# Selective-scan layer on one Trainium2 core: the stores of the scan's output are issued by ScalarE instead of SyncE

## What is computed

```python
def step(state, inp):
    d, b, c, uu = inp
    dA = jnp.exp(d[..., None] * A_neg[:, None, :, :])
    state = dA * state + (d * uu)[..., None] * b[:, :, None, :]
    y = jnp.einsum('kbcn,kbn->kbc', state, c)
    return (state, y)
```

## Time and profile before

| | us |
|---|---|
| median of 3 runs | 17231.57 |
| the profiled execution, its own time | 17236.15 |
| its span, first to last instruction | 17234.5 |

### The profile page before, as it was taken

How to read it: one execution, slowest core, us unless ns; L and a number is a source line. 1 busy time by engine, 2 the same in 40 slices (tenths; PEclk the granted TensorE clock), 3 DMA queues, 4 the chain that set the end, 5 groups by cost and what they waited for, 6 DMA issues and landing times. The chain is left out here.

```text
span 17234.5 us, 361490 instructions
## 1 busy us (share of the span) xinstructions
PE 12704.4 (74%) x127392; PEld 8742.7 (51%) x127392; DVE 11266.0 (65%) x10439; ACT 7765.1 (45%) x13769; POOL 6782.0 (39%) x3199
## 2 busy tenths in 40 slices
PE   7889999888999954454466666666666666667799
PEld 5666666666666632222244444444444444444477
DVE  5666666666666655555477777777777777775532
ACT  4444444444444434544455545554555545552200
POOL 1000000000000014423577777887778877772100
PEclk9999999999999977777677777777777777776799
DMA  5222222222222237766899999999999999998711
GB/s 124 65 57 58 59 59 53 66 56 66 59 59 59 53 106 186 179 153 159 209 233 233 234 230 233 235 235 234 236 232 235 237 228 232 233 230 222 197 39 40
DMA packets 2038805, 2633.89 MB, mean 153 GB/s; under 512 B 1083612, under 2 KB 1935324, under 8 KB 2013404
## 3 DMA queue, kind: packets, MB, share of 16 engines
q1 hardware_dynamic: 1991388, 2487.10, 59.5%
q0 software_dynamic: 12288, 86.71, 2.3%
q10 hardware_dynamic: 34944, 57.81, 1.2%
HBM read 2103.61 MB, written 556.32 MB: 154 GB/s over the span
## 5 line engine op out<-in xcount | busy, mean ns | idle before, releaser
L1731 DVE TENSOR_TENSOR_SCAN L2.h<-L2.ps,L2.db 128x912 f32<-128x912 f32 x2688 | 5515.0, 2056 | 1569.2 <-POOL L2.db L1587 1522.1
L1587 POOL TENSOR_TENSOR L2.db<-L2.du,L2.bt 128x896 f32<-128x896 f32 x2688 | 5580.1, 2096 | 1551.7 <-DMA L2.du<-du 1468.0
L1608 PE MATMUL L2.ps<-L2.dm,L2.wa 32*128 32x112 f32 x21504 | 2306.9, 346 | 2471.1 <-DVE L2.h L1731 2343.4
L1669 ACT ACTIVATE L2.ps<-L2.ps 128x896 f32<-128x896 f32 x2688 | 2424.5, 902 | 3503.4 <-PE L2.ps L1608 3501.6
L1608 PEld LDWEIGHTS L2.ps<-L2.dm,L2.wa 32*128 32x128 f32 x21504 | 1899.6, 246 | 3268.2 <-DVE L2.h L1731 2940.3
L1621 PE MATMUL L2.ps<-L2.h,L2.cd 128*8 128x96 f32 x50176 | 2575.6, 362 | 5.5 <-DVE L2.h L1731 5.5
L1621 PEld LDWEIGHTS L2.ps<-L2.h,L2.cd 128*8 128x8 f32 x50176 | 1439.4, 108 | 583.6 <-DVE L2.h L1731 5.6
L314 POOL TENSOR_TENSOR L1.x_res<-L1.x_res,L1.ob 96x3136 f32 (+1 forms) x16 | 95.4, 5977 | 2582.2 <-ACT L1.qv L457 2582.2
L314 POOL TENSOR_TENSOR L0.x_res<-L0.x_res,L0.ob 96x3136 f32 (+1 forms) x16 | 95.9, 6007 | 2367.8 <-ACT L0.qv L457 2367.8
L366 PE MATMUL L1.p_proj<-L1.xt,L1.w_hi 128*96 128x448 f32 x3024 | 826.4, 383 | 194.2 <-DVE L1.xt L560 167.5
L366 PE MATMUL L0.p_proj<-L0.xt,L0.w_hi 128*96 128x448 f32 x3024 | 826.3, 383 | 194.3 <-DVE L0.xt L560 167.6
(11 more groups left out here) (255 smaller groups left out, 19811.4 us busy)
## 6 DMA issues: line engine op xcount, KB each, us to landing
L2.du<-du SPq DMA_DIRECT2D x5376, 224.0 KB, 6.6
L2.dm<-d SPq DMA_DIRECT2D x896, 336.0 KB, 6.8
y<-L2.ysum SPq DMA_DIRECT2D x896, 84.0 KB
L0.left<-table SPq DMA_DIRECT2D x48, 1176.0 KB
L0.right<-table SPq DMA_DIRECT2D x48, 1176.0 KB
L1.left<-table SPq DMA_DIRECT2D x48, 1176.0 KB
L1.right<-table SPq DMA_DIRECT2D x48, 1176.0 KB
du<-L2p.work SPq DMA_DIRECT2D x64, 784.0 KB, 7.5
```

The lines of the kernel that those rows point to most:

```text
L1587: pool.tensor_tensor(db[:, n % RB, :, 2:ROW], du[:, n % RD, :].rearrange("p (c t) -> p c t", t=SPAN), row, ALU.mult)\
L1608: mm = pe.matmul(decays[n % RA][:, lo:lo + SPAN], wa[rows, u * QUAD + e, :], dm[rows, u * QUAD + e, :], start=True, stop=True)
L1669: act.activation(a, a, ACT.Exp).then_inc(a_ready, 1)
L1731: dve.tensor_tensor_scan(h[:, half, u * UNIT:(u + 1) * UNIT, :].rearrange("p c t -> p (c t)"), decays[n % RA], db[:, n % RB, :, :].rearran ...
```

## The change

The four stores of a half leave SP's program. ACT issues them on its own DMA queue at the end of its half-span, after the decay and the carry of unit 11 and ahead of `make_cd`. It first waits until its own seven copies have landed (`sum_out`). SP's wait on `sum_out` goes with the stores. Addresses, sizes and the semaphore `y_stored` stay as they are. The last store of the pass moves to the end of ACT's program.

```diff
@@ SP @@
-                    if u == 2 and earlier is not None:
-                        sp.wait_ge(sum_out, fills + (2 - FILLS))
-                        steady(sp)
-                        store_y(*earlier, half)
...
-            for half in range(2):
-                sp.wait_ge(sum_out, (DIRS * HALVES - 1 + half) * FILLS + 2)
-                store_y(DIRS - 1, NSPANS - 1, half)
@@ ACT @@
+            def store_y(k, s, half):
+                for q in range(4):
+                    at = s * SPAN + SPAN // 4 * q
+                    if k % 2:
+                        at = at * -1 + (TOK - SPAN // 4)
+                    rows = slice(at, at + SPAN // 4) if isinstance(s, int) else bass.ds(at, SPAN // 4)
+                    place = y_dram[k, :, rows, half * HALF:(half + 1) * HALF]
+                    act.dma_start(place, ysum[32 * q:32 * q + BATCH, half, :, :]).then_inc(y_stored[half], 16)
...
+                if not first:
+                    act.wait_ge(sum_out, before + (FILLS + 2))
+                    steady(act)
+                    if half:
+                        store_y(k, s, 0)
+                    elif begun:
+                        store_y(k - 1, NSPANS - 1, 1)
+                    else:
+                        store_y(k, act.snap(s - 1), 1)
                 if half == 0:
                     make_cd(k, s, before)
...
+            act.wait_ge(sum_out, DIRS * HALVES * FILLS + 2)
+            store_y(DIRS - 1, NSPANS - 1, 1)
```

More of the change, by code:

```diff
@@ L1499, in load_du, with half_span @@
                     sp.dma_start(du[:, slot, g * QUAD * SPAN:(g + 1) * QUAD * SPAN], src).then_inc(du_in[slot], 16)
[L1501 to L1510, removed]
+            def half_span(k, s, half, later, table):
                 units = count(sp, k, s, 2 * UNITS, half * UNITS)
-                fills = count(sp, k, s, 2 * FILLS, half * FILLS)
                 for u in range(UNITS):
@@ L1542, in span @@
             def span(k, s, last):
[L1543 to L1546, removed]
                 if last:
@@ L1550, in span @@
                     later = (k, s + 1) if isinstance(s, int) else (k, sp.snap(s + 1))
-                half_span(k, s, 0, earlier, (k, s), k if k and isinstance(s, int) and s == 0 else None)
-                half_span(k, s, 1, earlier, later, k + 1 if last and k + 1 < DIRS else None)
+                half_span(k, s, 0, (k, s), k if k and isinstance(s, int) and s == 0 else None)
+                half_span(k, s, 1, later, k + 1 if last and k + 1 < DIRS else None)
             sp.wait_ge(cleared, 1)
```

## The result

| | before | after |
|---|---|---|
| median of 13 runs | 17224.97 | 17148.3 |
| lowest to highest | 17209.45 to 17241.57 | 16911.1 to 17230.26 |
| the profiled execution, its own time | 17236.15 | 17109.6 |

The medians of the 13 runs have a ratio of 0.9955 and their means one of 0.9934 (0.990 to 0.997 with 95%); without the six runs that took over 1.5% more than the shortest, the ratio is 0.9895 (0.9862 to 0.9927), which favours a kernel whose runs scatter. The kernel is faster, by about 1% at most. The gain is 77 us in the medians and 126.6 us in the profiled executions, where 511 were forecast. A second thing is new: the runs of before lie within 0.2% of each other, those of after within 1.9%.

What follows compares the result with a forecast made beforehand. The du load was taken to bind, held by SP's queue blocked at stores. Loads 27.4 plus stores 1.8 gave 29.2 us a half-span, 2.3 less; 222 x 2.3 = 511 us off 17236 gave 16725, range 16300 to 17260.

Steps and rivals of the forecast that it cites:

- the bound and what held SP: Scan pass: du loads bind; SP's queue, blocked at stores, holds them back, 3.7 us behind a store.
- The third rival: Stores and loads: something both queues share is the block, so no change, 17236 us within 30; chance 0.12.
- ACT's side: ACT at a half's end: four issues, addresses and a wait take 2.3 us (1.4 to 3.4), costed at nothing.
- a sign: Trace of ACT's queue: its four store issues would take 2 to 3 us together.
- The cushion: ACT before unit 0's scan: 2.6 us of slack after a half 0; lateness at most 90 us over the pass.
- the store's own cost: DMA engines per half-span: the moved stores' bytes cost 0 to 2.4 us, taken as 1.8.
- The first rival: DMA engines: stores hidden at cost 0, half-span 27.4 us, program 16326 us; chance 0.15 for 16300 to 16590.
- the loads without the store: Half-span loads: 20.9 us for the mix at 245.5 GB/s plus 6.5 for eight du, together 27.4 us.
- the second rival: Smaller gain: stores cost 2.4 us or more, or ACT's hold eats part; chance 0.15 for 16860 to 17200 us.
- The fourth rival: The eight store engines: short writes between long reads lengthen loads; slower, 17570 us at 50 ns a packet; chance 0.11.
- the marks: Trace signs: du issues keep 2.85 us, slot waits rise, no share under 0.8, multiply's idle falls to about 960 us.

Runs made afterwards that it cites:

- even stores: Each y store takes 16 partitions, 8 of them unused rows: in the changed kernel (ACT's queue) 16419.08 us; in the kernel before (SP's queue) 17283.47 us.
- no stores: Changed kernel without any y store in the scan pass; ACT only counts the semaphore up and the next stage reads a stand-in: 16638.51 us, ratio 0.9666.
- half the bytes: Changed kernel with stores of 14 of the 28 tokens on 8 partitions, next stage reading a stand-in: 17346.7 us, ratio 1.0063.
- less in flight: Changed kernel, but SP waits for two more free slots, so at most four units of du are in flight instead of six: 17241.05 us, ratio 1.0011.
- waiting: Changed kernel, but SP waits once per half, ahead of its fifth unit, until ACT's stores have landed: 17483.54 us, ratio 1.0156.
- short reads: Kernel without stores, ACT issuing loads of the stores' size in 384-byte runs instead: 18097.28 us on 8 partitions, 17995.78 us on 16.
- tiny stores: Changed kernel with one token per store instead of 28, next stage reading a stand-in: 16604.54 us on 8 partitions, 16634.08 us on 16.

## Why the prediction was wrong in size

**Right: the bound and what held SP.** Before, the queue was blocked at the store. After, du's four issues keep their time beside the stores; SP's queue over a half-span, which answers the earlier trace rows:
```profile
14000.14 2.87 SPq L1499 DMA_DIRECT2D L2.du<-du  x4
...
14004.05 2.85 SPq L1499 DMA_DIRECT2D L2.du<-du  x4
...
14012.69 14.13 SPq L1499 DMA_DIRECT2D L2.du<-du  x10
...
14032.45 2.86 SPq L1499 DMA_DIRECT2D L2.du<-du  x4
```
The long entry in the middle contains waits for slots. The third rival, one block for both queues, is out, though 17148 us is only 88 us from its 17236. It had a page's rule beside it: by the Trainium skill (DMA: Bandwidth & Descriptors, section on issuing engines not being separate DMA queues) another issuing engine saves issue time alone. The gap between even stores on SP (17283) and on ACT (16419) disagrees, unless the time for which an issue stands blocked is counted as issue time: what the second queue saves is the blocking of the first, 5% of the time, though SP's unblocked issue time was never the bound.

**Right: ACT's side.** Its four issues were put at 2.3 us with bounds of 1.4 and 3.4. At the end of a half 0, in ACT's timeline, which answers the earlier trace rows:
```profile
10022.54 0.28 ACTq L1644 DMA_DIRECT2D y<-L2.ysum  x1
10022.94 0.20 ACT L1664 COPY L2.db<-L2.h 128x8 f32<-128x8 f32 x1
10023.00 2.85 ACTq L1644 DMA_DIRECT2D y<-L2.ysum  x3
10026.03 2.34 ACT L1651 ACTIVATE L2.cd<-L2.cc,L2.image 128x112 f32<-128x112 f32 x8 [2.90 <-issue]
10028.27 0.90 ACT L1657 ACTIVATE L2.ps<-L2.ps 128x896 f32<-128x896 f32 x1
```
From first start to last end it takes 3.1 us in the mean of all stores, within the bounds but over the 2 to 3 us named as a sign. The cushion held for the most part: the scan's idle time behind ACT rose from 29.2 us in sum (11.9 + 17.3) to 77.7 (40.4 + 37.3 above), 48 us in the whole pass where at most 90 were allowed.

**Within its bounds, but too high: the store's own cost.** It was bounded by 0 and 2.4 us and taken at 1.8. With even stores, twice the bytes, the half-span is 27.8 us; against the 27.4 worked out for the loads alone that leaves 0.4. The same 27.8 holds with the real stores while the engines are in step. No run gives the cost cleanly, since the kernel with no stores, 28.8 us, has its own late engine. The first rival's premise, hidden stores, comes nearest: it gave 16326, and 16419 was reached with even stores.

**Wrong: the loads without the store.** The step put du, dm, bt and cc at 245.5 GB/s, the rate of the earlier trace rows, and so at 20.9 us. After, the same mix runs at 214 in the mean of all half-spans: 5.13 MB / 214 is 24.0 us, 3.1 more. The packets that end from 10 to 22 us after a half-span's first scan carry, in GB/s (profiled runs, without the ends of each direction):

```
before 249, after 214, even stores 254, half the bytes 206, no stores 239, less in flight 246, waiting 247
```
With 24.0 for the mix, 6.5 for the other du and 0.4 for the stores that makes 30.9, and the half-span is 30.9 where 29.2 was forecast: the mix brings 3.1 us more and the stores 1.4 less. The difference of 1.7 us is 381 us over the pass, the amount by which the profiled execution falls short of the forecast (511 - 127 = 384). The row was read rightly, but it was a rate of engines that are in step, and what keeps them so, as far as the runs tell, is the very block that the change removes. I asked for each term what covers it, but not what keeps a rate as it is. What showed it in the trace of before was there: engines run dry at each store, and the store uses half of them.

**The rivals.** The time fell into the second rival's range, but not by its mechanism: neither the stores' price nor ACT's hold (48 us at most) ate the gain. The fourth rival had the place, the eight engines, and the mark that it was to be known by, a share near 1 with fewer GB/s. Its price was wrong: a turn between short writes and long reads would cost just as much on sixteen engines, where next to nothing is lost, and would fall in the stretch of the stores, which runs at 282 to 305 GB/s. Of the marks, no stretch looked at fell below a share of 1; the idle time ahead of the multiply came to 1347 where 960 was given (654 with even stores, 8588 to 14780 us).

**Shown, argued, open.** Shown: as many engines are late as a store has partitions (8, 12), also in loads that land after the stores; a half-span is 27.8 us in step and 30.5 to 32 out of step within one execution; emptying the queue, or making the stores even, restores step and rate. Argued only: that the eight late engines are the eight that store, since the trace doesn't name the engine of a landing; that the lag makes the loads slow and not the slow loads the lag; that a full queue keeps the lag alive until the six slots cap it. The even stores also give y sixteen rows in memory in place of eight. Full stores on 8 partitions into such a y weren't run; with tiny stores the two layouts are alike (16605 and 16634 us). Open: why the memory or the engines serve loads at 241 instead of 257 to 279 GB/s when they are out of step; why half the bytes cost more than all; why one engine lags with no stores; why short reads cost what short writes don't. The records hold no view of an engine's own backlog, so these were not settled.

## What to carry to other kernels

When a small transfer blocks a queue of large ones, moving it to another engine's queue can pay. In this kernel it paid in full only with the transfer on all 16 DMA engines, like the large ones. So try its partition count padded to 16, even with rows that nobody reads (here twice the bytes, and 17148 became 16419 us, against 17225 before). This was measured for short writes; short reads were slow either way. When a change removes a stall, ask what the stall kept in order, and don't carry over a rate that was measured behind it. A DMA share near 1 with a lower GB/s is a reason to look at when each engine's part of one load lands, and a kernel whose runs suddenly scatter by 2% is another.

## What the hardware showed that I hadn't expected

- DMA engines fall out of step and stay there: in loads issued 15 to 20 us after the first store, which land after the stores, eight engines are 2.7 to 3.6 us behind the first; loads then run at 241 GB/s instead of 257 to 279 at the same share.
- The state comes and goes within one execution, with nothing in the program that changes: 1.8 to 4.0 us of spread over seven half-spans.
- Twice the bytes on twice the engines were 4.3% faster (16419 against 17148), half the bytes on the same engines 1.2% slower (17347).
- Without any store one engine lands its part 4.2 us after the first, and the kernel is 1.3% slower (16639) than with even stores of full size.
- Short reads on a second queue lengthen a half-span to about 36 us in the profiled runs, where writes of that shape on 16 partitions leave it at 27.8.
